# First attention stage of a two-layer decoder kernel: another order at its start and in its last group

## The reference

```python
def lora_linear(x, W, b, Bm, Am):              # Bm: 16 x 256, Am: 256 x 16
    out = jnp.einsum('bld,od->blo', x, W) + b
    upd = jnp.einsum('blr,or->blo', jnp.einsum('bld,rd->blr', x, Bm), Am)
    return out + 0.5 * upd
q, k, v = (split(lora_linear(x, ...)) for each)   # 16 heads of 16
scores = jnp.einsum('bhqd,bhkd->bhqk', q, k) * 16 ** -0.5
attn = jax.nn.softmax(scores, axis=-1)
out = jnp.einsum('bhqk,bhkd->bhqd', attn, v)
x = x + lora_linear(out, Wo, bo, Bo, Ao)       # x in the calls above: layernorm(x)
```

## Time and profile before

| | us |
|---|---|
| median of 3 runs | 1025.43 |
| the runs | 1019.35, 1025.43, 1025.58 |
| the profiled execution, its time | 1027.5 |
| its span | 1025.7 |
| end of the stage's last matmul | 184.4 |
| TensorE busy in the span | 964.2 (94%) |
| VectorE busy | 648.9 (63%) |
| ScalarE busy | 483.2 (47%) |
| GpSimd busy | 241.7 (24%) |

### The profile page before, as it was taken

The page is one execution under the profiler, slowest core; times in us unless marked ns, Lnnn a source line. Parts: engine busy times, 40 slices in busy tenths (PEclk is TensorE's granted clock), DMA queues, the critical chain, the costliest instruction groups (busy, mean ns, idle before and its releaser), DMA issues.

```text
span 1025.7 us, 19821 instructions
## 1 busy us (share of the span) xinstructions
PE 964.2 (94%) x7443; PEld 831.4 (81%) x7443; DVE 648.9 (63%) x1377; ACT 483.2 (47%) x1612; POOL 241.7 (24%) x238
## 2 busy tenths in 40 slices
PE   7899998898987999999999999999999998899877
PEld 5677776898866898888889888898889877777757
DVE  5578886599876576544644446444464467777854
ACT  3778885432233555444444434444444454444421
POOL 3355774410331132111111111111111123110000
PEclk9899996999999999999999999999999999999979
DMA  8000000000111122100000000000000231000002
GB/s 299 5 2 3 2 2 1 23 1 1 55 50 44 62 63 63 52 1 1 2 1 2 1 2 1 1 1 1 1 1 1 62 131 63 1 2 1 1 1 83
DMA packets 12076, 27.89 MB, mean 27 GB/s; under 512 B 1936, under 2 KB 7088, under 8 KB 11344
## 3 DMA queue, kind: packets, MB, share of 16 engines
q1 hardware_dynamic: 11264, 26.42, 7.5%
q10 hardware_dynamic: 720, 0.20, 0.1%
HBM read 24.52 MB, written 2.10 MB: 26 GB/s over the span
## 4 chain that ended last, share of the span: by engine, by line
PE 62%; DVE 3%; ACT 2%; issue 1%; POOL 0%; DVEq 0%; ACTq 0%
PE bank L42 14%; PE bank L43 13%; PE bank L44 13%; PE bank L1387 6%; PE bank L1336 5%; PE bank L1377 3%; PE bank L1881 2%; PE bank L1894 2%; PE bank L2332 1%; PE bank L1871 1%; PE bank L1860 1%; PE bank L143 1%; PE bank L2390 1%; PE bank L2367 1%; DVE li_rden L2087 1%
## 5 line engine op out<-in xcount | busy, mean ns | idle before, releaser
L1311 POOL TENSOR_TENSOR wa_prob<-wa_prob,wa_rsum 128x512 f32<-128x512 f32 x64 | 75.7, 1183 | 431.2 <-DVE wa_rsum L1562 431.2
L42 PE MATMUL bank<-norm_xT_hi,wide_hi 128*128 128x512 f32 x256 | 106.7, 417 | 3.3 <-ACTq L1524 3.3
L1467 ACT ACTIVATE wa_prob<-wa_prob,wa_negmax 128x128 f32<-128x128 f32 x256 | 99.9, 391 | 16.7 <-DVE wa_negmax L1551 16.4
L1596 DVE TENSOR_TENSOR le_w_or_z_lo<-bank,le_w_or_z_hi 128x512 fp32r<-128x512 f32 x64 | 44.3, 691 | 94.8 <-ACT le_w_or_z_hi L1508 94.1
L44 PE MATMUL bank<-norm_xT_hi,wide_lo 128*128 128x512 f32 x256 | 101.9, 398 | 0.0
L43 PE MATMUL bank<-norm_xT_lo,wide_hi 128*128 128x512 f32 x256 | 101.8, 398 | 0.0
L1488 ACT COPY wa_v<-bank 128x512 f32<-128x512 f32 x64 | 37.5, 586 | 127.5 <-PE bank L44 127.4
L521 ACT ACTIVATE v_or_conv<-bank,la_negmax 128x128 f32<-128x128 f32 x256 | 90.7, 391 | 5.0 <-PE bank L359 3.7
L1557 DVE COPY wa_k<-bank 128x512 f32<-128x512 f32 x64 | 44.3, 691 | 63.9 <-PE bank L44 63.8
L1475 ACT COPY wa_q<-bank 128x512 f32<-128x512 f32 x64 | 37.6, 588 | 99.0 <-PE bank L44 99.0
L281 POOL TENSOR_TENSOR v_or_conv<-v_or_conv,la_rsum 128x512 f32<-128x512 f32 x64 | 66.6, 1041 | 67.4 <-DVE la_rsum L589 67.3
(11 more groups left out here) (312 smaller groups left out, 2502.8 us busy)
## 6 DMA issues: line engine op xcount, KB each, us to landing
h_or_w<-in_wide_w SPq DMA_DIRECT2D x11, 512.0 KB, 4.4
li_em_w<-in_em_w SPq DMA_DIRECT2D x1, 4096.0 KB, 12.4
x<-in_x SPq DMA_DIRECT2D x4, 512.0 KB, 5.0
lc_kt<-in_ctx_rev SPq DMA_DIRECT2D x1, 2048.0 KB, 10.4
lc_toep<-in_toeplitz SPq DMA_DIRECT2D x1, 2048.0 KB, 14.7
wa_v<-in_wide_w SPq DMA_DIRECT2D x4, 512.0 KB, 7.9
out_x<-x SPq DMA_DIRECT2D x8, 256.0 KB, 2.9
li_kt<-in_ctx_rev SPq DMA_DIRECT2D x1, 1536.0 KB, 7.6
```

Source lines behind the costliest of these rows:

```text
L42: nc.tensor.matmul(out, a[0], b[0], start=start, stop=False, skip_group_check=True)
L1311: nc.gpsimd.tensor_tensor(prob[:, s], prob[:, s], rsum[:, s, :].unsqueeze(2).to_broadcast([P, G, P]), ALU.mult).then_inc(prob_ok, 1)
L1467: last = nc.scalar.activation(prob[:, s, j, :], prob[:, s, j, :], ACT.Exp, bias=negmax[:, s, j:j + 1], scale=SCALE, accum_out=sums[:, s, j ...
L1596: nc.vector.tensor_tensor(z[1][:, t % 2, :], b_z[:, :], z[0][:, t % 2, :].bitcast(F32), ALU.subtract).then_inc(z_lo, 1)
```

## The change

At the start: the first quarter of x is loaded ahead of the LoRA tables instead of behind them. The tables are laid out with each matrix's 16 rows at partition 0, 32, 64 or 96, padded with zero rows to 32, so each grows from 64 KB to 128 KB. The LoRA products go matrix by matrix for each half, on four row blocks, with one semaphore increment after the last. VectorE folds q and k, makes what the q and k products need, and only then folds v and o. The bias product moves from ahead of the q product to behind the first scores, and the first scores move ahead of the values. GpSimd's four additions of the bias to group 0 move from ahead of step 0 into steps 2 to 5.

In all groups the layer norm statistics come one step earlier. In the last group `o_rest` moves ahead of `row_max`.

```diff
-        lora_a = sb("lora_a", [R, 4, D])
-        lora_b = sb("lora_b", [R, 4, D])
+        lora_a = sb("lora_a", [P, D])
+        lora_b = sb("lora_b", [P, D])
-        STATS_AT, RSTD_AT, APPLY_AT, BIAS_AT = 3, 5, 7, 10
+        STATS_AT, RSTD_AT, APPLY_AT, BIAS_AT = 2, 4, 6, 10
-        ORDER = (2, 0, 1, 3)
+        ORDER = (0, 1, 2, 3)
 # SyncE
+            load_x(sp, 0)
             sp.dma_start(lora_b[:], io["l0_b"]).then_inc(lora_loaded, 16)
             sp.dma_start(lora_a[:], io["l0_a"]).then_inc(lora_loaded, 16)
-            load_x(sp, 0)
             sp.dma_start(w_raw[:], io["l0_w"]).then_inc(loaded, 16)
 # GpSimd
-            pool.wait_ge(bias_ok, 1)
-            for j in range(G):
-                add_bias(0, j)
             normalise(0)
             for n in range(N - 1):
                 g, u = divmod(n, U)
                 normalise(n + 1)
...
+                if 2 <= n < 2 + G:
+                    if n == 2:
+                        pool.wait_ge(bias_ok, 1)
+                    add_bias(0, n - 2)
 # TensorE
-            for n in ORDER:
-                for c in range(DC):
-                    last = nc.tensor.matmul(b_s[n][:, c * D:(c + 1) * D], lora_b[:, n, c * P:(c + 1) * P],
-                                            lora_a[:, n, :], start=True, stop=True)
-                last.then_inc(w_ps, 1)
+            for c in range(DC):
+                for n in range(4):
+                    rows = slice(32 * n, 32 * n + 32)
+                    last = nc.tensor.matmul(b_s[n][:, c * D:(c + 1) * D], lora_b[rows, c * P:(c + 1) * P],
+                                            lora_a[rows, :], start=True, stop=True)
+            last.then_inc(w_ps, 1)
             pe.wait_ge(loaded, 16 * NLOAD)
             for c in range(DC):
                 turn_x(0, c, b_p[c])
             for m in range(DC):
                 q_or_k(0, m, 0, b_p[m], q_ps)
...
+            scores(0)
+            scores(2)
             pe.wait_ge(w_f32, 4)
...
             last.then_inc(bias_ps, 1)
             pe.wait_ge(w_lo, 3)
             for half in range(2):
                 pe.wait_ge(k_ok, half + 1)
                 values(0, half, b_p[half])
-            scores(0)
-            scores(2)
 # ScalarE
-                if m == 1:
+                if m == 0:
                     for c in range(DC):
                         norm.hi_chunk(act, 0, c, b_p[c], xT[0][0])
+            exps(0)
+            exps(1)
             act.wait_ge(v_zero, 1)
             for half in range(2):
                 keep_v(0, half, b_p[half])
-            exps(0)
-            exps(1)
 # VectorE, opening
+            fold(0)
+            fold(1)
...
                 if n == 1:
                     for c in range(DC):
                         norm.lo_chunk(dve, 0, c, b_p[c], *xT[0])
+                if n == 2:
+                    fold(2)
+                    fold(3)
                 dve.wait_ge(w_hi, n + 1)
                 nc.vector.tensor_tensor(w[1][:, n], w_raw[:, n], w[0][:, n].bitcast(F32), ALU.subtract)\
                     .then_inc(w_lo, 1)
 # VectorE, steps
                 if n + 1 < N:
                     inverse_sums(n + 1)
+                if g >= NG - 1:
+                    o_rest_due(n)
                 if n + 3 < N:
                     row_max(n + 3)
...
-                b = batch_due(n, HI_AT)
-                if b is not None:
-                    o_rest(b)
+                if g < NG - 1:
+                    o_rest_due(n)
                 if n < N:
                     keep_probT(n)
```

More of the change, by code:

```diff
@@ L445, in _ @@
                 turn_x(0, c, b_p[c])
+            pe.wait_ge(norm.s_lo, DC * norm.split(0))
+            pe.wait_ge(w_lo, 2)
+            for m in range(DC):
+                q_or_k(0, m, 0, b_p[m], q_ps)
+            for m in range(DC):
+                pe.wait_ge(q_ok, m + 1)
+                q_or_k(0, m, 1, b_p[m], k_ps)
+            scores(0)
+            scores(2)
             pe.wait_ge(w_f32, 4)
@@ L451, in _ @@
             last.then_inc(bias_ps, 1)
-            pe.wait_ge(norm.s_lo, DC * norm.split(0))
-            pe.wait_ge(w_lo, 2)
-            for m in range(DC):
-                q_or_k(0, m, 0, b_p[m], q_ps)
             pe.wait_ge(w_lo, 3)
-            for m in range(DC):
-                pe.wait_ge(q_ok, m + 1)
-                q_or_k(0, m, 1, b_p[m], k_ps)
             for half in range(2):
@@ L600, in o_rest, with o_rest_due @@
                                         oT[0][:, b % 2, :, :].bitcast(F32), ALU.subtract).then_inc(ot_lo, 1)
+            def o_rest_due(n):
+                b = batch_due(n, HI_AT)
+                if b is not None:
+                    o_rest(b)
             def update(b):
@@ L625, in extra, with fold @@
                     add_skip(pr, (u,))
+            def fold(m):
+                n = ORDER[m]
+                dve.wait_ge(w_ps, 1)
+                nc.vector.scalar_tensor_tensor(w_raw[:, n], b_s[n][:, :].rearrange("p (c o) -> p c o", c=DC),
+                                               LORA, w_raw[:, n], ALU.mult, ALU.add).then_inc(w_f32, 1)
             dve.wait_ge(pr.x_loaded[0], 16)
@@ L629, in _ @@
             dve.wait_ge(loaded, 16 * NLOAD)
-            for m, n in enumerate(ORDER):
-                dve.wait_ge(w_ps, m + 1)
-                nc.vector.scalar_tensor_tensor(w_raw[:, n], b_s[n][:, :].rearrange("p (c o) -> p c o", c=DC),
-                                               LORA, w_raw[:, n], ALU.mult, ALU.add).then_inc(w_f32, 1)
+            fold(0)
+            fold(1)
             for e in range(2):
@@ L643, in _ @@
                     .then_inc(w_lo, 1)
-            dve.wait_ge(bias_ps, 1)
-            nc.vector.tensor_tensor(out_bias[:], b_t[:, 0:D], out_bias[:], ALU.add).then_inc(bias_ok, 1)
             dve.wait_ge(pr.x_loaded[1], 16)
@@ L650, in _ @@
             inverse_sums(0)
+            dve.wait_ge(bias_ps, 1)
+            nc.vector.tensor_tensor(out_bias[:], b_t[:, 0:D], out_bias[:], ALU.add).then_inc(bias_ok, 1)
             row_max(2)
@@ L2617 @@
     r["l0_w"] = np.stack([chunks(a[f"L0_attn_W{n}"][order[n]].T) for n in qkvo], axis=1)
-    r["l0_a"] = np.stack([a[f"L0_attn_A{n}"][order[n]].T for n in qkvo], axis=1)
-    r["l0_b"] = np.stack([a[f"L0_attn_B{n}"] for n in qkvo], axis=1)
+    lora = np.zeros((2, 4, 32, D), np.float32)
+    for i, n in enumerate(qkvo):
+        lora[0, i, 0:16] = a[f"L0_attn_A{n}"][order[n]].T
+        lora[1, i, 0:16] = a[f"L0_attn_B{n}"]
+    r["l0_a"], r["l0_b"] = lora.reshape(2, P, D)
     r["l0_qk_bias"] = np.stack([a[f"L0_attn_b{n}"][rows].reshape(DC, P).T for n in "qk"], axis=1)
```

## The result

| | median us | runs | from to |
|---|---|---|---|
| before | 1022.56 | 20 | 1019.35 to 1025.58 |
| changed | 1015.5 | 20 | 1011.38 to 1023.87 |

The ratio is 0.9936, with a 95% interval of 0.9918 to 0.9954: faster by 0.64%, which is under the 1% that the prediction asked for before it would say faster, so its case "same" came. The forecast of 1014 lies 1.5 off and the range holds the time, but the drop is 7.1, and the sum had put it at 4.9 + 1.7 + 5.9 = 12.5. Two things are mixed in this: with more runs the old median came down by 2.9, and the change gave less than the sum said.

A forecast was written before the change was run, and what follows sets the result against it. TensorE's own list was taken to set the pace in the first stage's middle, leaving the opening and last group to gain. 1027.5 - 4.9 - 1.7 - 5.9 = 1015.0, less half the 2.1 offset, gave 1014 us; range 1009 to 1021.

The forecast's parts named there:

- case "same": Whole kernel: a time not told apart from no change, faster starting only below 1015.2 us; chance 0.46.
- the sum: First stage: gains of 4.9 us in the opening, 1.7 from last-group idlings and 5.9 from the last group's clock.
- Opening: the chain of steps: Opening: earlier folds, q product, scores and step 0 gain 2.8 us, the low stretch behind step 0 another 2.1.
- my halving: Opening, LoRA products: two row blocks run at once, so 3.6 us instead of 7.19.
- rival B: Opening: LoRA products do not overlap, folds start at 12.5 and 2.7 us are lost, 1017.7 or 1017; chance 0.08.
- Last group, idlings: Last group: rest of the result ahead of the maxima saves 1.3 us in step 53 and 0.4 in step 49.
- Last group, clock: Last group, steps 54 to 60: without the 1.66 us idling TensorE's clock stays up, saving 5.9 us, bounds 0 and 5.9.
- A: Last group: the clock falls all the same, so 5.9 us stay in, 1020.9 or 1020 less half the offset; chance 0.24.
- C: Opening and last group: step 0 stays at 32 and the clock falls at both places, about 1025; chance 0.04.
- D: Last group: VectorE waits for ScalarE's cast, maxima and exps slip 5.6 us, clock falls from step 48, 1034; chance 0.04.
- starting time: Whole kernel: the profiled execution's 1027.5 us, less half of its 2.1 us offset above the median.

The follow-up runs named there:

- f2_one_block: Changed kernel with the LoRA tables at 16 partitions again and the eight products one after the other; 1019.46 us, ratio 0.9955 to the kernel before.
- e2_last: Kernel before with only the last-group part added (statistics one step earlier, rest of the result ahead of the maxima), old opening kept; 1018.15 us, ratio 0.9949.
- e4_before_fill: Kernel before with two added matmuls, results unread, ahead of each transposition of steps 50 to 63; 1027.46 us, ratio 1.0032.
- g4_before_again: Kernel before, unaltered, run again for a second profile; 1022.37 us, ratio 0.9993.
- e1_opening: Changed kernel with its last-group part undone (statistics and rest of the result as before), new opening kept; 1017.91 us, ratio 0.9967 to the kernel before.
- g3_stats_only: Changed kernel with the rest of the result behind the maxima again, earlier statistics kept; 1015.36 us, ratio 0.9940 to the kernel before.
- f4_after_again: Changed kernel, unaltered, run again for a second profile; 1015.81 us, ratio 0.9929 to the kernel before.
- g2: Changed kernel with the statistics at their old steps again, rest of the result still ahead of the maxima; 1020.56 us, ratio 0.9976 to the kernel before.
- f1: Changed kernel with values and their ScalarE copies ahead of the first scores again; 1019.77 us, ratio 0.9955 to the kernel before.
- g1: Changed kernel with two banks for transposed probabilities in steps 51 to 63, plus two added matmuls ahead of the q product; 1012.15 us, ratio 0.9900.
- f3: Changed kernel with transposed probabilities of steps 51 to 63 put into two banks in turn; 1014.25 us, ratio 0.9908 to the kernel before.

## Why the prediction was right and where it was not

**Opening: the chain of steps right.** First fold 9.8, measured 9.87; q product 13.9, measured 14.04; scores 23.45, measured 23.58; step 0 29.95, measured 29.50; step 2 35.5, measured 34.95. The LoRA products were put at 3.6 and took 2.09, which is 7.19 divided by 3.44; as their end at 8.3 lay ahead of the first fold, this cost nothing, as said. The Trainium skill's factor of 3.07 for four row tiles (TensorE: Matmul & The Clock Gate, "Measured speedup vs the span model") had given an estimate of 2.3, and the trace is nearer to that than to my halving. f2_one_block shows the item's worth: without overlap the opening loses 3.4 at step 2 (38.11 instead of 34.7), where rival B said 2.7.

**Opening: the gain was read off one draw.** Four profiles have the old opening and their step 2 is at 40.33, 36.22, 38.40 (e2_last) and 37.78 (e4_before_fill), 38.2 on average; the seven with the whole new one lie between 34.27 and 34.99, 34.7 on average. That is a gain of 3.5, not 4.9. Two things differ among the old ones. The rate of the q product rises 6.4 us into it in the earlier trace rows and at 4.3, 3.0 and 0.3 us in e2_last, e4_before_fill and g4_before_again. And behind the idling of 2.6 the way from step 0 to step 2 takes 7.57 in the earlier trace rows and 6.0 to 6.2 in the others. The profile that I had was the worst of the four in both. The new opening removes that idling, and its step 2 hardly varies. The whole runs agree: the ratio of e1_opening is a gain of 3.4 us (1.3 to 5.5).

**Last group, idlings: wrong.** The sum had 1.7, of it 0.4 in step 49. The sentence that failed is "They serve a step three ahead, so I count nothing". It looked at whom the maxima serve, and not at what stands behind them on VectorE: the copy of the transposed probabilities, for which TensorE's next transposition waits. Exchanging two operations ahead of it cannot bring it forward; it can only add the wait for ScalarE's cast, 0.57 in step 57. g3_stats_only prices the exchange at +0.85. In step 53 the sum had 1.3. The weighing's wait did fall, from 1.66 to 0.15, but the next transposition waits 0.77 instead of 0.17, so 0.9 is left of it; the statistics alone give as much (0.70 + 0.17 = 0.87 in g3_stats_only, against 1.83), and the text had credited it to the move of the rest.

**Last group, clock: the mechanism right, the size mis-set.** The term was 5.9 for steps 54 to 60, and where the clock stayed up its rate came: in f4_after_again these six steps take (163.26 - 151.46) / 6 = 1.97 each, instead of 2.96. Steps 48 to 63 by length of their low stretch: 28.64 with none (f4, e2), 30.10 with 3.4 (f2), 31.65 with 6.8 (after, and 31.67 in e1), 35.33 with 17 (before, and g4). So a microsecond at the low level costs about 0.4 here, and the full 17 cost 6.7. What failed is "I take all of it": the term took the stretch as certain before and gone after. The text's reason, "the one long idling is the only thing that tells this stretch from the one ahead of it", did not hold: the clock also fell behind idlings of 0.46 and 0.77 (after) and of 0.48 and 0.77 (g2), and with these same idlings it stayed (f4). Profiles with the old last group had 17, 17 and 7 us of low stretch (before, g4, e1), those with the new one 7, 0, 0, 7 and 3.4 (after, f4, e2, f1, f2). The averages, 13.6 and 3.4, differ by 10.2, worth 4.1 us at 0.4 each. That is an estimate from three and five profiles; the ratio of e2_last says 5.2 (3.2 to 7.2) for this part. With the opening's 3.5 it makes 7.6, and the ratio of the whole change says 1022.56 x 0.0064 = 6.5, between 4.7 and 8.4. That the last-group part gains is shown by e2_last; that it gains by fewer and shorter low stretches is argued from these profiles, and no run here fixed the clock without adding work.

**Rivals.** A (the clock falls all the same) is partly true: the prediction's own sign for it, a clock of 0.50 in the last group, is in the changed kernel's profile (0.51, for 7 us instead of 17), and f1 and f2 have low stretches there too. How often it falls is not known: 4 of the 20 runs lie above 1020, at mean clocks of 0.967 and 0.968, but no profile of them shows in which stage. It belonged in the sum as a share, not beside it as another world. The rule of the Trainium skill that the prediction named there (TensorE: Matmul & The Clock Gate, "Part 4: PE-mode transpose"), that transpositions do not count as activity, could not be told apart here: the last group kept 1.00 for 29 us in f4 and g3, but it holds scores and weighings as well. B, C and D did not come; D's mechanism, VectorE standing still for the cast, exists with 0.57 us in step 57, a tenth of the 5.6 that it was priced at.

**The numbers.** 1014 came out near 1015.5 because two errors nearly cancelled: 12.5 - 7.1 = 5.4 too much gain, and a starting time (1027.5 less 1.05) 3.9 above the later median of 1022.56. That is luck. The prediction also read the 6.1 us by which 1019.35 lies below the other two runs as the price of the low stretch; the openings of the kernel before alone differ by 4.1 at step 2, so that reading is not shown.

## What to carry to other kernels

Before two operations on an in-order engine are exchanged, look at the third one behind them and who waits for it; if that wait ends last, the exchange moves an idling and saves nothing. Where, as in this last group, the same idlings came once with a low clock and once without, take the price of the clock as a share of runs, and draw several profiles before a low stretch is entered at full length. Whether a few throwaway matmuls in a wait ahead of dense ones pay is open: g1 is one profile, and its interval does not part it from f3.

## What the hardware showed that was not expected

The moment at which the q product's rate rises is itself a draw. In the nine profiles that have the new load order and nothing added ahead of the product it came 3.0 to 6.4 us into it, at 20.2 in the changed kernel's; in the four of the old opening 6.4, 4.3, 3.0 and 0.3 us in. With two added matmuls of 1.9 us together ahead of it (g1) the rate was high from the start (14.26). That fits a rise that follows what TensorE did before, but g4_before_again did as well without them, so it is not shown. The granted clock in the windows reads 1.00 in all these cases from the start, and only the distance between matmuls, 0.43 or 0.23, tells the level there. With some matmuls added in one stage, TensorE waited 2.0 us for its own instructions some 420 us later, in both profiles that have them and in none of the other twelve, and the clock fell behind that too.
